# Unread products and a moved quantiser in a chunk scan, attention waits by parts, expert results by partition, activation tables fetched earlier

## What is computed

```python
# layer 0, attention part: per sequence and head a 4-row "fast weight" W_in, W_out, updated chunk by chunk (16 tokens)
def step(carry, xs):
    W_in, W_out = carry
    q_t, k_t, v_t, lr_t = xs
    k_h = softmax(einsum('blhd,bDhd->blhD', k_t, W_in)) * lr_t[..., 1:]
    q_h = softmax(einsum('blhd,bDhd->blhD', q_t, W_in))
    qk = einsum('bqhD,bkhD->bhqk', q_h, k_h) * mask
    o_t = einsum('bqhD,bDhd->bqhd', q_h, W_out) + einsum('bhqk,bkhd->bqhd', qk, v_t)
    W_out = W_out + einsum('bnhD,bnhd->bDhd', k_h, v_t)
    for _ in range(2):
        g_out = -attn(W_in, k_t, v_t)
        g_in = -attn(W_out, v_t, k_t)
        W_in, W_out = W_in - lr_in * g_in, W_out - lr_out * g_out
    return (W_in, W_out), o_t
```

## Time and profile before

| | |
|---|---|
| median of 3 runs | 925.34 us (924.12 to 926.57) |
| profiled execution | 919.76 us |
| its span | 918.0 us |
| mean granted TensorE clock | 0.821 of full |
| PE busy | 658.5 us (72%) |
| DVE busy | 642.9 us (70%) |
| ACT busy | 341.4 us (37%) |
| POOL busy | 362.8 us (40%) |
| DMA | 41.28 MB, mean 45 GB/s |

### The profile page before, as it was taken

The page is one execution under the profiler, slowest core; times in us unless marked ns, Lnnn a source line. Parts: engine busy times, 40 slices in busy tenths (PEclk is TensorE's granted clock), DMA queues, the critical chain, the costliest instruction groups (busy, mean ns, idle before and its releaser), DMA issues. The chain is left out here.

```text
span 918.0 us, 19134 instructions
## 1 busy us (share of the span) xinstructions
PE 658.5 (72%) x6928; PEld 505.2 (55%) x6928; DVE 642.9 (70%) x1809; ACT 341.4 (37%) x794; POOL 362.8 (40%) x511
## 2 busy tenths in 40 slices
PE   1677787778767565789999988306578773496896
PEld 1265565556544444677777868304356552254586
DVE  3774688887886664577777774385664668699886
ACT  1654111221212144456666653122213442374521
POOL 1450344443442245535555505642761665020111
PEclk9978756665667787699999999856698997598999
DMA  2000000000000400021000024426437552300001
GB/s 55 1 1 1 14 2 2 2 3 2 2 2 2 74 6 6 1 81 42 9 12 10 10 67 120 143 57 97 135 104 194 159 169 74 87 0 1 1 12 35
DMA packets 66291, 41.28 MB, mean 45 GB/s; under 512 B 11889, under 2 KB 64193, under 8 KB 66209
## 3 DMA queue, kind: packets, MB, share of 16 engines
q1 hardware_dynamic: 62432, 32.43, 14.4%
q0 software_dynamic: 3776, 7.78, 2.3%
HBM read 26.72 MB, written 13.47 MB: 44 GB/s over the span
## 5 line engine op out<-in xcount | busy, mean ns | idle before, releaser
L1734 ACT ACTIVATE l1a_weights<-l1a_score,l1a_low_top 128x128 f32<-128x128 f32 (+1 forms) x256 | 90.3, 425 | 37.7 <-DVE l1a_low_top L1766 32.5
L1766 DVE TENSOR_REDUCE l1a_low_top<-l1a_score 128x2 f32<-128x512 f32 (+1 forms) x96 | 66.1, 689 | 53.4 <-PE l1a_score L1643 52.6
L1598 POOL TENSOR_TENSOR l1a_q_of<-l1a_q_rows,l_quad_of 128x1024 fp32r<-128x1024 f32 x32 | 59.8, 1894 | 38.2 <-ACT l1a_q_rows L1723 38.2
L1640 PE MATMUL l1a_score<-l1a_k_rows,l1a_q_of 128*128 128x128 f32 (+1 forms) x256 | 53.3, 313 | 17.9 <-ACT l1a_weights L1734 10.6
L1789 DVE COPY l1a_weightsT<-l1a_flip 128x512 f32<-128x512 f32 x96 | 65.4, 681 | 0.9 <-PE l1a_flip L1678 0.8
L1278 POOL DMA_INDIRECT l_done<-l2e_done,l2r_rows x47 | 46.2, 983 | 41.1 <-DVE l2e_done L2484 40.5
L1678 PE MATMUL l1a_flip<-eye,l1a_weights 128*128 128x128 f32 x384 | 59.5, 279 | 0.1
L1640 PEld LDWEIGHTS l1a_score<-l1a_k_rows,l1a_q_of 128*128 128x128 f32 x256 | 38.5, 202 | 32.9 <-ACT l1a_weights L1734 20.4
L1678 PEld LDWEIGHTS l1a_flip<-eye,l1a_weights 128*128 128x128 f32 x384 | 47.5, 145 | 3.1 <-issue 0.8
L828 POOL TENSOR_TENSOR l0s_shared<-l0s_own,l0s_grown 128x512 f32<-128x512 f32 x16 | 18.1, 1132 | 75.3 <-ACT l0s_grown L818 75.3
L1261 POOL DMA_INDIRECT l_rows<-l2r_sent,l2r_slot x32 | 30.9, 967 | 27.7 <-DVE l2r_slot L1245 15.0
(11 more groups left out here) (550 smaller groups left out, 1938.1 us busy)
## 6 DMA issues: line engine op xcount, KB each, us to landing
l2e_wgu<-in_l_wgu SPq DMA_DIRECT2D x47, 128.0 KB, 2.1
l1e_w<-in_l_w SPq DMA_DIRECT2D x46, 128.0 KB, 2.4
l_rows<-l2r_rows SPq DMA_DIRECT2D x1, 3055.0 KB
l2e_wd<-in_l_wd SPq DMA_DIRECT2D x47, 64.0 KB, 2.0
l2r_rows<-l_rows SPq DMA_DIRECT2D x3, 780.0 KB, 6.1
l2e_mixed<-l_done SPq DMA_DIRECT2D x8, 256.0 KB, 4.4
l_rows<-l1r_rows SPq DMA_DIRECT2D x1, 1483.5 KB, 10.9
l1r_rows<-l_rows SPq DMA_DIRECT2D x3, 387.0 KB, 4.2
```

Source lines behind the costliest of these rows:

```text
L1598: nc.gpsimd.tensor_tensor(q_of[i][:, 4 * g:4 * g + 4, :], rep(q_rows[:, g, :], 1, 4), rep(lat.quad_of[:, 0, 0:4], 2, L), ALU.mult).then_in ...
L1640: nc.tensor.matmul(bank[:, n * width:(n + 1) * width], q_of[i][:, h, tile * P:(tile + 1) * P], k_rows[i][:, h // 4, 0:width], start=n == 0 ...
L1734: last = nc.scalar.activation(weights[s % 2][:, n * width:(n + 1) * width], score[s % 2][:, n * width:(n + 1) * width], ACT.Exp, bias=low_ ...
L1766: nc.vector.tensor_reduce(low_top[:, s % 2, 0:len(heads)], score[s % 2][:, :].rearrange("p (h k) -> p h k", k=key_tiles * P), AX.X, ALU.ma ...
```

## The change

- `l0_scan`, TensorE: `fill(count, bank)` multiplies the identity by the first 128 tokens of `xnT` into the last quarter of a PSUM bank, `count` times; nothing reads that. Called 1, 2, 2, 1 and 5 times in a step, always ahead of a wait. The wait for `grown_kept` moves to the top of the step, because the fills write into that bank.
- Quantiser: `quantise` and `choose` leave the scan; one `quantise(c)` of the same seven operations on 128x512 is called four times in `l0_project`, twice between `invert` and `normalise`, twice at the end. The scale's transfer, maximum and reciprocal move too.
- `Route`: a token's result goes to the place `p * 16 + t` in `done_dram` in place of `t * 128 + p`, so that each partition `p` reads four consecutive rows in one piece of 2 KB in `load_results`, where it read four pieces of 512 B.
- `l1_attention`: in the first sequence the scores of step `s` (0 to 3) wait for `q_staged` of `s + 1`, not for four at step 0.
- Three activations on one column whose result nothing reads: a square root ahead of the wait for the variance in `l1_experts`, a square root at the head of `l3_norms`, a GELU at the head of `l3_tail`.

```diff
@@ l0_project, VectorE
                 invert(0)
+                dve.wait_ge(scale_in, 16)
+                order.then(nc.vector.tensor_scalar_max(scale[:, :], scale[:, :], 1e-5))
+                order.then(nc.vector.reciprocal(inv[:, :], scale[:, :]))
+                quantise(0)
                 normalise(0, K)
                 invert(1)
+                quantise(1)
                 normalise(1, Q)
+                quantise(2)
+                quantise(3)
+                def quantise(c):
+                    quant = fast.quant[:, c * CH:(c + 1) * CH]
+                    order.then(nc.vector.tensor_scalar(level[:, :], core.xnT[:, c * CH:(c + 1) * CH], inv[:, :], ROUND, ALU.mult, ALU.add))
+                    order.then(nc.vector.tensor_scalar(level[:, :], level[:, :], -ROUND, LEVELS, ALU.add, ALU.min))
+                    order.mark(nc.vector.tensor_scalar(spare[:, :], level[:, :], -LEVELS, scale[:, :], ALU.max, ALU.mult))
+                    order.then(nc.vector.tensor_scalar(quant, level[:, :], LIMIT, LIMIT, ALU.mult, ALU.min))
+                    order.mark(nc.vector.tensor_scalar(finite[:, :], spare[:, :], 0.0, 0.0, ALU.mult, ALU.is_equal))
+                    order.then(nc.vector.tensor_scalar_max(quant, quant, -LIMIT))
+                    order.then(nc.vector.copy_predicated(quant, finite[:, :], spare[:, :]))
@@ l0_scan, TensorE
+                def fill(count, bank=grown_ps):
+                    for _ in range(count):
+                        nc.tensor.matmul(bank[:, 3 * P:4 * P], core.eye[:, :], core.xnT[:, 0:P], start=True, stop=True)
                 for c in range(NCK):
                     if c:
+                        pe.wait_ge(grown_kept, c)
+                        fill(1)
                         pe.wait_ge(here_ready, c)
...
                     if c:
                         give_results(c - 1)
+                    fill(2)
                     pe.wait_ge(ready["own"], c + 1)
                     last = add(OLD, 2, fast.v_toks, c, both(own[c % 2][:, 0, :, :].rearrange("p (g h) i -> p g (h i)", g=2)))
+                    fill(2)
                     pe.wait_ge(ready["out"], c + 1)
...
                     last.then_inc(out_summed, 1)
+                    fill(1)
                     pe.wait_ge(old_ready, c + 1)
...
                     if c < LAST:
+                        fill(5, out_ps)
                         pe.wait_ge(ready["in"], c + 1)
@@ l0_scan, VectorE
                     if c >= 2:
                         centre(c - 2)
-                    quantise(c)
                     dve.wait_ge(out_summed, c + 1)
...
-                    choose(c)
                     if c >= 2:
                         sum_squares(c - 2)
@@ Route
-            pool.iota(self.sent[i][:, :, D:D + 1].bitcast(I32), [[P, NT], [1, 1]], base=i * N, channel_multiplier=1)
+            pool.iota(self.sent[i][:, :, D:D + 1].bitcast(I32), [[1, NT], [1, 1]], base=i * N, channel_multiplier=NT)
@@ load_results
-                rows = self.done_dram[i * N + c * CH:i * N + (c + 1) * CH, :]
-                sp.dma_start(out[:, c * TPC:(c + 1) * TPC, :], rows.rearrange("(t p) d -> p t d", p=P)).then_inc(self.loaded[c], 16)
+                rows = self.done_dram[i * N:(i + 1) * N, :].rearrange("(p t) d -> p t d", p=P)[:, c * TPC:(c + 1) * TPC, :]
+                sp.dma_start(out[:, c * TPC:(c + 1) * TPC, :], rows).then_inc(self.loaded[c], 16)
@@ l1_attention, scores
-                    if s == 0:
+                    if first:
+                        if s == 0:
+                            pe.wait_ge(rows_taken, 4)
+                        if s < 4:
+                            pe.wait_ge(q_staged, s + 1)
+                    elif s == 0:
                         pe.wait_ge(rows_taken, (b + 1) * 4)
                         pe.wait_ge(q_staged, (b + 1) * 4)
-                        if not first:
-                            pe.wait_ge(v_staged, b * 2)
+                        pe.wait_ge(v_staged, b * 2)
@@ l1_experts, ScalarE
                 act.wait_ge(cleared, 1)
+                nc.scalar.activation(idle[:, :], eps_col[:, :], ACT.Sqrt)
                 act.wait_ge(var_ready, 1)
@@ l3_norms, ScalarE
+                nc.scalar.activation(idle[:, :], core.head_of[:, 0:1], ACT.Sqrt)
                 four.take(act, banks)
@@ l3_tail, ScalarE
+                nc.scalar.activation(idle[:, :], core.head_of[:, 0:1], ACT.Gelu)
                 loads.wait(act)
```

More of the change, by code:

```diff
@@ L375, in l0_project @@
         rate_wide = sb("rate_wide", [P, NCK, 8, CK])
+        scale, inv, level, spare = sb("scale", [P, 1]), sb("inv", [P, 1]), sb("level", [P, CH]), sb("spare", [P, CH])
+        finite = local.enter_context(nc.sbuf_tensor("l0p_finite", [P, CH], I32))
+        LEVELS, ROUND, LIMIT = 127.0, 1.5 * 2.0 ** 23, 1e4
         near, far = (local.enter_context(nc.psum_tensor(f"l0p_{n}", [P, BANKS, CH], F32)) for n in ("near", "far"))
@@ L395, in l0_project, with _ @@
         with nc.Block() as block:
+            @block.sync
+            def _(sp):
+                sp.dma_start(scale[:, :], act_scale_dram.partition_broadcast(P)).then_inc(scale_in, 16)
             @block.gpsimd
@@ L642, in l0_scan @@
         turned = pair("turned", [P, 2, P])
-        scale, inv, bias = sb("scale", [P, 1]), sb("inv", [P, 1]), sb("bias", [P, D])
-        level, spare, mean, square = sb("level", [P, P]), sb("spare", [P, P]), sb("mean", [P, H]), sb("square", [P, H, HD])
-        finite = local.enter_context(nc.sbuf_tensor("l0s_finite", [P, P], I32))
-        LEVELS, ROUND, LIMIT = 127.0, 1.5 * 2.0 ** 23, 1e4
+        bias, mean, square = sb("bias", [P, D]), sb("mean", [P, H]), sb("square", [P, H, HD])
         w_ps = ps("w", [P, 4, CH])
@@ L688, in _ @@
             def _(sp):
-                sp.dma_start(scale[:, :], act_scale_dram.partition_broadcast(P)).then_inc(scale_in, 16)
                 sp.dma_start(fast.tern_int[:, :], ternary_dram).then_inc(tern_in, 16)
@@ L939, in _ @@
                         order.mark(nc.vector.tensor_scalar_add(fast.w_tern[:, :], fast.tern_int[:, :], -1.0))
-                        dve.wait_ge(scale_in, 16)
-                        order.then(nc.vector.tensor_scalar_max(scale[:, :], scale[:, :], 1e-5))
-                        order.then(nc.vector.reciprocal(inv[:, :], scale[:, :]))
                     if c >= 2:
                         centre(c - 2)
-                    quantise(c)
                     dve.wait_ge(out_summed, c + 1)
@@ L1866, in l1_experts @@
         rstd, minus, eps_col = sb("rstd", [P, NT]), sb("minus", [P, NT]), sb("eps_col", [P, 1])
+        idle = sb("idle", [P, 1])
         turned, up, down = ([ps(f"{n}{i}", [P, CH]) for i in range(2)] for n in ("turned", "up", "down"))
@@ L2640, in l3_norms @@
         std, left, both = (sb(n, [P, NT]) for n in ("std", "left", "both"))
-        eps_col = sb("eps_col", [P, 1])
+        eps_col, idle = sb("eps_col", [P, 1]), sb("idle", [P, 1])
         turned = [local.enter_context(nc.psum_tensor(f"l3a_turned{i}", [P, CH], F32)) for i in range(2)]
@@ L2858, in l3_tail @@
         w1, w2, bias1, bias2 = (loads[n] for n in ("w1", "w2", "bias1", "bias2"))
[L2859 removed]
+        hidden, idle = pair("hidden", [P, FK, CH]), sb("idle", [P, 1])
         level, grain = pair("level", [P, TPB * HB, BLK]), sb("grain", [P, TPB * HB, BLK])
```

24 lines of the change are left out of this document (6 added, 18 removed).

## The result

The changed kernel takes 894.32 us, median of four runs (890.46 to 897.48), against 924.73 for the kernel before: a ratio of 0.9673 with a 95% interval of 0.9641 to 0.9704. The forecast was 899.0 within 890 to 912; the gain is 30.4 us where the sum had 26.3. The profiled execution has a span of 890.6 us, 27.4 under that of before. In some executions of the kernels with unread products TensorE's clock stays at its low level for 40 us of layer 2, which adds some 15 us; the ratios leave the runs out that are longer by that much, the medians do not.

What follows compares the result with a forecast made beforehand. It took layer 0's scan, a closed PE, VectorE and ScalarE chain mostly at TensorE's low clock, as the largest loss. Scan −17.9, projection +0.8, attention −5.0, results −1.1 and tables −3.1 gave −26.3: 899.0 us, range 890 to 912.

Steps and rivals of the forecast that it cites:

- The clock is held: Layer 0's scan: main assumption that full-tile unread products hold TensorE's clock at 2.4 GHz; scan window near 1.00.
- A step at the upper level, 10.5 us: Layer 0's scan: a high-clock step takes 10.5 us, so fifteen steps take 157.5 instead of 176.6, −19.1.
- The fills cost 0.1 us per step, and 1.0 for the start: Layer 0's scan: unread products charged +1.5 in all, plus +1.0 for steps before the clock is up.
- The quantiser's gain: Layer 0's scan: seven VectorE operations leave each step, 0.97 us inside the 10.5; mask w_old at 4.84, not 5.81.
- The rivals: Six other outcomes: clock partly held 0.14, slower 0.07, moved work shows 0.10, change misfires 0.07, better 0.09, nothing 0.03.
- The projection, +0.8: Layer 0's projection: four quantiser sets added, first two free, last two end at 92.3; +0.8, between 0 and +2.
- Attention by parts, −5.0: Layer 1's attention: first scores need one masking, not four, and start at 366.2 instead of 371.26; −5.0.
- Expert results, −1.1: Read-back of expert results in 2 KB pieces: −0.8 in layer 1, −0.3 in layer 2.
- Tables ahead, −3.1: Three idle activations take table loads off the chain: layer 1 −1.3, layer 3 −0.8, tail −1.0.

Runs made afterwards that it cites:

- small_tiles: The changed kernel with its 11 unread products per step made by tiles of 32 rows and 32 columns; 978.79 us in a single run.
- few: The changed kernel with 7 unread products per scan step in place of 11; 910.46 us, ratio 0.9850.
- fills_only: The kernel before with the 11 unread products per step and the earlier wait for the grown tile alone, quantiser still in the scan; 937.42 us, ratio 1.0149.
- quant_only: The kernel before with the quantiser alone moved to the projection, no unread products; 920.61 us, ratio 0.9963.
- held: The kernel before with 18 unread products per step, seven more than the change's 11, and the quantiser still in the scan; 931.61 us, ratio 1.0099.
- rest_only: The kernel before with all of the change except the scan's and the projection's edits; 914.62 us, ratio 0.9902.
- best: The changed kernel with the old results order, five unread products at the projection's end, eight for two before the first own sums; ratio 0.9666, median 901.65 us.

## Why the prediction was right, point by point

*The clock is held.* Right, after one step: 0.96 over the scan. It was named as an assumption that no row showed; `small_tiles` shows on what it hung, the size of the tiles, `few` that there was little to spare, and `fills_only` that without the other half it fails.

*A step at the upper level, 10.5 us.* Measured 10.49, and part by part: 3.65 to the out sums (3.65), 4.84 to the mask w_old (4.84), 3.90 to the in sums (3.9), 0.74 to w_here (0.74), 1.01 to the next reduction (1.0). Reading the one step of before that ran at the upper level, with the rest from a low one, was enough.

*The fills cost 0.1 us per step, and 1.0 for the start.* In steps at the upper level they cost nothing. Instead the first step is 12.24 us and one, in which the clock is 0.85, 11.43. The terms were 2.5 together, the measured loss against fifteen steps of 10.49 is 2.7.

*The quantiser's gain.* Here the step was wrong, though the total was not. I took the mask w_old at 5.81 us to be held by the quantiser. But TensorE's out sums end there only at 204.43 + 1.99 = 206.42, and the mask starts at 206.59: the quantiser held it for 0.1 us, the slow out sums for the rest, and `quant_only` gained 0.1 us a step. The place to read the price was the step of the earlier trace rows, whose out sums end at 241.52:

```profile
242.56 0.42 DVE L889 TENSOR_TENSOR l0s_w_old<-l0s_w_ps,l_w_mask 128x256 f32<-128x256 f32 x1
...
243.03 0.44 PE L704 MATMUL l0s_in_ps<-l_rows,l0s_w_old 128*32 128x32 f32 x16 [1.51 <-DVE l0s_w_old L889]
```

There the quantiser alone holds the mask, by 0.97 us, and TensorE, whose clock is low again (0.44 us, against 0.33 in the changed kernel), idles 1.51 us. So 0.97 was the right size at the upper clock, by a row that I had not used. It is paid only with the other half done. I priced nothing for the three operations behind `ready["in"]`; `fills_only` and `held` measure 1.61 for all seven, the copy behind POOL's product being the part that I left out. The rivals had no case for the two halves needing each other, and `fills_only` shows that a forecast of the fills alone by the same sum would have had the wrong sign.

*The projection, +0.8.* The first three sets cost nothing, as worked out; the fourth ends at 92.32 (92.3). The later start is 1.0, near the term. But the first reduction is 2.8 us later: 1.8 is the clock, which falls during the scan's first products. The sum had nothing for that, and the runs show that it doesn't follow from the edit alone: the same idle of 1.9 us is left without a fall in four other executions.

*Attention by parts, −5.0.* Measured −5.0: masking at 347.57, keys done at 350.06, scores at

```profile
350.11 1.11 PE L1658 MATMUL l1a_score<-l1a_k_rows,l1a_q_of 128*128 128x128 f32 x4 [0.69 <-ACT l1a_k_rows L1741]
```

*Expert results, −1.1.* Wrong: 0 in layer 1 and +1.3 in layer 2 by the means of fourteen profiled executions. In the changed kernel's own the two are −0.6 and +0.4 against before, so its total shows little of it. The Trainium skill's "DMA: Bandwidth & Descriptors", section "Why small descriptors are slow (HBM only)", by which joining is worth it only at 256 B or less, was nearer: it gives nothing for 512 B; it does not give the loss.

*Tables ahead, −3.1.* Layer 1's root comes 1.7 us after the last statistics instead of 3.1, −1.3 as forecast. Layer 3's comes −1.4, where I took 0.8. In the tail the load stands where TensorE starts:

```profile
822.40 1.28 ACT L2973 ACT_TABLE_LOAD   x1 [0.27 <-PEq L179]
...
822.44 9.05 PE L2924 MATMUL l3t_up<-l_hT,l3m_w 128*128 128x512 f32 x16 [1.12 <-PEq L179]
...
824.59 0.69 ACT L2982 ACTIVATE l3t_hidden<-l3t_up,l3m_bias 128x512 f32<-128x512 f32 x1 [0.69 <-PE l3t_up L2924]
```

The first GELU starts 2.15 us after TensorE, 2.48 before: −0.3 in place of −1.0. But the two compare different clocks: here the stage's first products run at the low level, in the kernel before at the upper. `rest_only` has the edit and the upper level, and its GELU starts 1.37 us after TensorE:

```profile
846.72 7.88 PE L2911 MATMUL l3t_up<-l_hT,l3m_w 128*128 128x512 f32 x16 [1.12 <-PEq L179]
...
848.09 1.32 ACT L2969 ACTIVATE l3t_hidden<-l3t_up,l3m_bias 128x512 f32<-128x512 f32 x2
```

Over all profiled executions it is 1.4 with the edit and 2.5 without at the upper level, 2.1 or 2.2 and 3.4 at the low one. So the edit is worth 1.1 to 1.3 us, as forecast, and the clock took 0.8 of it back. In the two profiled executions the three come to −3.0. The 2.66 us per switch of the Trainium skill ("ScalarE: Activation LUTs", section "What ACT_TABLE_LOAD costs") would have given −8; nothing of that size is seen.

*Not in the sum:* the end. The last products run at the low level now (chain of waits, from 882.93):

```profile
882.93 1.28 PE l3t_turned L2943 x6
...
885.13 1.65 PE l3t_result L2955 x6
```

against 0.89 and 0.94 us for the same two before: 1.1 us, by where the clock stood. No edit need be behind it: `fills_only`, `quant_only` and `held`, whose last layer is that of the kernel before, end 1.1 us later too, counted from the last product of `l3t_down` (26.7 to 26.8 us, 25.7 before). And layer 2's −2.3 and the attention's −2.5 us belong to no step. Without these two the stretches that the sum spoke of, end included, give −22.6 against its −26.3: the total came out as near as it did with their help. From the first to the last score of the attention, four of the nine profiled executions with the parted wait take 172.6 to 172.8 us, one 173.7, four 174.5 or 174.6, and the five without it 174.0 to 174.3. The four of 174.5 are the same that have the low stretch in layer 2 later. Among the others the parted wait goes with up to 1.5 us less; how it would do that is left open.

## What to carry over

Filling an engine's gaps to hold its clock pays only when nothing else reopens them: measure what the other engines do at the upper clock, since work that hid behind a slow TensorE comes onto the chain as soon as it is fast, and price both halves of such an edit together and each alone. Use full-sized tiles, put them where a trace shows idle time, and count both sides: here 4 products fewer per step cost 10 us of scan and 6 more cost 9. Read the price of work beside a chain from a step that already runs at the speed you are forecasting. And compare two executions only where their clock stood alike, or over several: two of the terms above looked wrong by 0.8 and 1.8 us for no other reason.

## What the runs showed of the hardware

- TensorE busy 99% of a 221 us stretch with small tiles was granted a clock of 0.53, where the same number of products with 128x128 tiles gave 0.96 at 91% busy.
- TensorE at the low level for 40 us, 20.00 and 18.96 of 20 us busy, in work that other executions did at 1.00 (`best`, windows at 655.5 and 675.5). It costs some 15 us, and came only in kernels with unread products in the scan. The cause is open.
- The same idle of 1.9 us ahead of the scan's first products was followed by a fall of the clock within the sixteen products in three profiled executions and not in four.
- A predicated copy of 128x128 on VectorE took 0.30 or 0.31 us where a product of POOL on 128x512 started 0.09 us behind it, and 1.05 or 1.06 where that product had started 0.23 us ahead of it.
- Reading 256 KB back from DRAM in pieces of 2 KB was no faster than in pieces of 512 B, and over eight such transfers 1.3 us slower (means of six and eight profiled executions).
